# Cross-attention in a decoder: scores contracted over 64 rows on each half of the array, keys spread by ScalarE in place of GpSimd

## The reference

```python
x = x + attn_stack(layernorm(x))
# cross-attention: q from layernorm(x), k and v from ctx (16, 128, 128)
qh = (q @ Wq + bq)   # (16, heads 16, 128, 16)
kh = (k @ Wk + bk)
vh = (v @ Wv + bv)
scores = einsum('bhqd,bhkd->bhqk', qh, kh) * 16 ** -0.5
x = x + (softmax(scores) @ vh, heads joined) @ Wo + bo
x = x + experts(layernorm(x))
```

## Time and profile before

| | us |
|---|---|
| median of 3 runs | 3431.5 (3430.92 to 3431.95) |
| span of the profiled execution, first to last instruction | 3428.6 |
| cross-attention in it, from the first load to the last update | 2851.2 to 3101.5 |

### The profile page before, as it was taken

How to read it: one execution, slowest core, us unless ns; L and a number is a source line. 1 busy time by engine, 2 the same in 40 slices (tenths; PEclk the granted TensorE clock), 3 DMA queues, 4 the chain that set the end, 5 groups by cost and what they waited for, 6 DMA issues and landing times. The chain is left out here.

```text
span 3428.6 us, 44182 instructions
## 1 busy us (share of the span) xinstructions
PE 3029.2 (88%) x11560; PEld 2029.0 (59%) x11561; DVE 2711.6 (79%) x8902; ACT 1927.6 (56%) x2995; POOL 1323.7 (39%) x1039
## 2 busy tenths in 40 slices
PE   5698989898989898999899989998999976998995
PEld 4465656565656565666566655665566644776553
DVE  8879888988898889888988898889888834763111
ACT  4566666666666666666666666666666622442221
POOL 5325343534353435343534353435443323333002
PEclk9899999999999999999999999999999987997998
DMA  4001100100011001000100010001000001003312
GB/s 102 17 1 24 25 16 18 24 25 16 18 24 25 16 18 24 25 16 18 24 25 16 18 24 25 16 18 24 18 24 4 1 0 49 0 0 131 100 40 74
DMA packets 212286, 93.22 MB, mean 27 GB/s; under 512 B 146792, under 2 KB 207984, under 8 KB 212048
## 3 DMA queue, kind: packets, MB, share of 16 engines
q1 hardware_dynamic: 209408, 83.30, 9.6%
q0 software_dynamic: 2640, 7.21, 0.6%
HBM read 80.24 MB, written 10.22 MB: 26 GB/s over the span
## 5 line engine op out<-in xcount | busy, mean ns | idle before, releaser
L350 PE MATMUL PS<-XTHI,WHI 128*128 128x512 f32 x1536 | 672.6, 438 | 38.1 <-DVE EK L654 27.9
L285 POOL TENSOR_TENSOR INV<-INV,CE 128x512 f32<-128x512 f32 x256 | 305.9, 1195 | 984.1 <-DVE INV L697 984.1
L646 DVE SCALAR_TENSOR_TENSOR RK<-RK,EK 128x128 f32<-128x128 f32 x1024 | 599.6, 638 | 28.7 <-ACT RK L515 0.5
L351 PE MATMUL PS<-XTLO,WHI 128*128 128x512 f32 x1536 | 610.7, 398 | 0.0
L352 PE MATMUL PS<-XTHI,WLO 128*128 128x512 f32 x1536 | 609.9, 397 | 0.0
L398 PE MATMUL Y<-ATT,WO 128*128 128x512 f32 x1024 | 468.5, 612 | 59.8 <-POOL ATT L289 59.4
L398 PE MATMUL Y<-H,W2S 128*128 128x512 f32 x1024 | 465.9, 609 | 51.9 <-DVE R L708 50.4
L289 POOL TENSOR_TENSOR ATT<-INV,CC 128x512 f32<-128x512 f32 x256 | 316.7, 1237 | 195.5 <-PE Y L398 177.9
L398 PEld LDWEIGHTS Y<-ATT,WO 128*128 128x128 f32 x1024 | 197.7, 196 | 301.0 <-issue 298.2
L350 PEld LDWEIGHTS PS<-XTHI,WHI 128*128 128x128 f32 x1536 | 291.4, 190 | 133.2 <-issue 42.3
L398 PEld LDWEIGHTS Y<-H,W2S 128*128 128x128 f32 x1024 | 197.0, 195 | 290.4 <-issue 227.2
(11 more groups left out here) (195 smaller groups left out, 5440.7 us busy)
## 6 DMA issues: line engine op xcount, KB each, us to landing
STAGE<-L_attn_Wk SPq DMA_DIRECT2D x128, 64.0 KB, 2.1
STAGE<-L_attn_Wv SPq DMA_DIRECT2D x128, 64.0 KB, 2.1
STAGE<-L_attn_Wq SPq DMA_DIRECT2D x128, 64.0 KB, 2.1
WO<-L_attn_Wo SPq DMA_DIRECT2D x8, 1024.0 KB, 5.5
W2S<-L_attn_W SPq DMA_DIRECT2D x8, 1024.0 KB, 6.1
STAGE<-L_attn_W SPq DMA_DIRECT2D x64, 128.0 KB, 3.7
RAW<-L_ffn_r_gate SPq DMA_DIRECT2D x8, 512.0 KB, 3.5
RAW<-L_ffn_r_up SPq DMA_DIRECT2D x8, 512.0 KB, 3.6
```

The source lines that it names most:

```text
L285: nc.gpsimd.tensor_tensor(r3, r3, spread(CE[:, e, :], SEQ), ALU.mult).then_inc(att_s, 1)
L350: nc.tensor.matmul(out, whi[:, kc, :], xhi[:, kc, :], start=(kc == 0), stop=False)
L351: nc.tensor.matmul(out, whi[:, kc, :], xlo[:, kc, :], start=False, stop=False)
L646: ins = nc.vector.scalar_tensor_tensor(RK[:, p, seq(b)], RK[:, p, seq(b)], 0.0, EK[:, p, seq(b)], ALU.add, ALU.add, accum_out=SUMK[:, p, b ...
```

## The change

The scores now contract 64 rows, the four heads of one half: rows 0 to 63 with the first half of KX, rows 64 to 127 with the second, as two matmuls on two halves of the array's rows. KX so needs four copies of the keys instead of eight, and each row keeps its own head's copy among its four. ScalarE writes these copies straight from PSUM, as scale x keys + scale x bias, where the scale is a column of ones and zeros (PAIR, one column for each of four heads) and the bias a masked one (BKP). GpSimd's products, KT and the large mask are gone; VectorE makes PAIR from a small mask of GpSimd's, and BKP once the biases have landed. The scores now wait for ScalarE's keys and queries themselves.

```diff
+GROUPS = 2
+GH = CH // GROUPS
+GROUP = P // GROUPS
...
-        KT = sb("XKT", [P, 2, KD, P])
-        KX = sb("XKX", [P, 2, CH, SEQ])
+        KX = sb("XKX", [P, 2, KD, GH, SEQ])
...
-        S = ctx.enter_context(nc.psum_tensor("XS", [P, 2, CH * SEQ], F32))
+        S = ctx.enter_context(nc.psum_tensor("XS", [P, KD, GROUPS, GH * SEQ], F32))
...
-            def apart(i, j, c):
-                u = (2 * i + j) * KD + c
-                pool.wait_ge(kt, 2 * i + (j + 1))
-                if not (type(i) is int and u < 2):
-                    pool.wait_ge(s_mm, u - 1)
-                nc.gpsimd.tensor_tensor(KX[:, c, :, :], bcast(KT[:, j, c, :], CH), MASK[:, :, :], ALU.mult).then_inc(kx, 1)
...
             def scores(b, j, c):
                 u = b * KD + c
-                pe.wait_ge(kx, u + 1)
+                pe.wait_ge(kt, b + 1)
+                pe.wait_ge(qt, b + 1)
                 if not (type(b) is int and u < 2):
                     pe.wait_ge(sh, u - 1)
-                for hf in range(2):
-                    ins = nc.tensor.matmul(S[:, c, hf * 512:(hf + 1) * 512], QT[:, j, c, :],
-                                           KX[:, c, hf * 4:(hf + 1) * 4, :].rearrange("p h s -> p (h s)"),
-                                           start=True, stop=True)
+                for i in range(GROUPS):
+                    rows = slice(i * GROUP, (i + 1) * GROUP)
+                    ins = nc.tensor.matmul(S[:, c, i, :], QT[rows, j, c, :],
+                                           KX[rows, j, c, :, :].rearrange("p h s -> p (h s)"), start=True, stop=True)
                 ins.then_inc(s_mm, 1)
...
             def qk(b, j):
                 act.wait_ge(qk_mm, b + 1)
                 for c in range(KD):
-                    ins = nc.scalar.activation(KT[:, j, c, :], A[:, (2 + c) * P:(3 + c) * P], ACT.Identity,
-                                               bias=BK[:, c:c + 1])
+                    for h in range(GH):
+                        ins = nc.scalar.activation(KX[:, j, c, h, :], A[:, (2 + c) * P:(3 + c) * P], ACT.Identity,
+                                                   scale=PAIR[:, h:h + 1], bias=BKP[:, c, h:h + 1])
                 ins.then_inc(kt, 1)
...
+            dve.wait_ge(own_set, 2)
+            nc.vector.tensor_reduce(PAIR[:, :], OWN[:, :].rearrange("p (i h) -> p h i", h=GH), AX.X,
+                                    ALU.max).then_inc(pair_set, 1)
             prepare(0)
+            dve.wait_ge(pair_set, 1)
+            dve.wait_ge(bias_in, 64)
+            nc.vector.tensor_tensor(BKP[:, :, :], spread(BK[:, :], GH), bcast(PAIR[:, :], KD), ALU.mult).then_inc(bkp_set, 1)
             dve.wait_ge(r0, 1)
             dve.wait_ge(prep, 3)
             normed(0, 0)
             normed(1, 1)
             prepare(1)
-            dve.wait_ge(bias_in, 64)
             values(0, 0)
```

More of the change, by code:

```diff
@@ L872, in cross_attention @@
         BOX = sb("XBO", [P, D])
-        MASK = sb("XMASK", [P, CH, SEQ])
+        OWN = sb("XOWN", [P, CH])
+        PAIR = sb("XPAIR", [P, GH])
+        BKP = sb("XBKP", [P, KD, GH])
         HALF = sb("XHALF", [P, SEQS])
@@ L899, in cross_attention @@
         w_in, bias_in = (sem(n) for n in ("xw_in", "xbias_in"))
-        set0, ones_set, v0, r0, mask_set, kx = (sem(n) for n in ("xset0", "xones_set", "xv0", "xr0", "xmask_set", "xkx"))
+        set0, ones_set, v0, r0, own_set, pair_set, bkp_set = (
+            sem(n) for n in ("xset0", "xones_set", "xv0", "xr0", "xown_set", "xpair_set", "xbkp_set"))
         prep, z, mx, sh, rd, o, v1, ob, upd = (
@@ L928, in _ @@
             nc.gpsimd.memset(HALF[:, :], -0.5).then_inc(set0, 1)
-            nc.gpsimd.memset(MASK[:, :, :], 1.0).then_inc(set0, 1)
+            nc.gpsimd.memset(OWN[:, :], 1.0).then_inc(set0, 1)
             nc.gpsimd.memset(V1[:, :, :, XK:XK + 1], 1.0).then_inc(ones_set, 1)
             pool.wait_ge(set0, 2)
[L933 to L937, removed]
+            nc.gpsimd.affine_select(out=OWN[:, :], in_=OWN[:, :], compare_op=ALU.is_ge, fill=0.0, base=0,
+                                    pattern=[[-XK, CH]], channel_multiplier=1).then_inc(own_set, 1)
+            pool.wait_ge(own_set, 1)
+            nc.gpsimd.affine_select(out=OWN[:, :], in_=OWN[:, :], compare_op=ALU.is_ge, fill=0.0, base=XK - 1,
+                                    pattern=[[XK, CH]], channel_multiplier=-1).then_inc(own_set, 1)
             def rstd(k):
@@ L947, in _ @@
             rstd(0)
-            pool.wait_ge(mask_set, 2)
-            def apart(i, j, c):
-                u = (2 * i + j) * KD + c
-                pool.wait_ge(kt, 2 * i + (j + 1))
-                if not (type(i) is int and u < 2):
-                    pool.wait_ge(s_mm, u - 1)
-                nc.gpsimd.tensor_tensor(KX[:, c, :, :], bcast(KT[:, j, c, :], CH), MASK[:, :, :], ALU.mult).then_inc(kx, 1)
-            apart(0, 0, 0)
-            apart(0, 0, 1)
-            rstd(1)
[L960 to L965, removed]
+            rstd(1)
         def step(i, j):
@@ L1135, in _ @@
             inputs(0, 0)
+            act.wait_ge(bkp_set, 1)
             qk(0, 0)
@@ L1160, in shifted @@
                 dve.wait_ge(s_mm, u + 1)
-                scores = S[:, c, :].rearrange("p (h s) -> p h s", h=CH)
+                scores = S[:, c, :, :].rearrange("p i (h s) -> p (i h) s", h=GH)
                 nc.vector.tensor_reduce(MX[:, c, :], scores, AX.X, ALU.max).then_inc(mx, 1)
```

## The result

The change makes the kernel slower: 3483.4 us median (3479.0 to 3488.4) beside 3431.2 us for the kernel before on the same chip, a ratio of 1.016 with a 95% interval of 1.014 to 1.018.

A forecast was written before the change was run, and what follows sets the result against it. It took a loop closing through TensorE, ScalarE and VectorE, 12.80 us a sequence, as the bound. Terms 34.5 - 6 + 1.5 - 0.4 + 7 = +36.6 us gave 3468; range 3442 to 3502, with 0.19 outside.

The forecast's parts named there:

- ScalarE's evictions, +34.5: Key evictions in the cross-attention loop, eight in place of two, lengthen the path by 2.3 us in each of 15 sequences.
- The choice of a second operand that costs as much as the first: Each key eviction's scale column adds 95 ns, as the bias does, so the eight stand 0.35 us apart.
- The scores, -6: Score matmuls on 64 rows free 0.43 us ahead of the projection, 14 times; the other chunk frees nothing.
- The choice of three pass times: A chunk's four score passes take 1.29 us, only the middle two overlapping; bounds 0.86 and 1.72.
- the slack at the projection: 0.54 us between the turned output's copy and the projection, while TensorE streams scores; the most the scores could free.
- The rival of a faster kernel: TensorE is the true bound and both score chunks run in 0.86 us: -27.5 us, 3404; chance 0.08.
- Ahead of the loop, +1.5: The masked bias on VectorE waits for the bias vectors, so the values come later: 1.5 us, bounds 0 and 2.5.
- GpSimd and VectorE, 0: Dropping GpSimd's products speeds VectorE's normalisation, but VectorE then waits for the projection: no time gained.
- The clock, +7: TensorE's new wait after narrow matmuls brings clock falls in three sequences of four, not two: +7 us, bounds -14 and +14.
- Rival 2: The clock falls for most of the loop, two falls a sequence: +71 us, 3502; stretch 3485 to 3520, chance 0.19.
- the forecast's own stretch: The main forecast's interval for the changed kernel's time, 3458 to 3485 us, chance 0.50.
- the signs that were to show the forecast wrong: Transposes still some 4.6 us after the first, pace set outside this loop, or granted clock in the loop below 0.8.

The follow-up runs named there:

- kernel 2: The kernel before plus six ScalarE activations with scale and bias columns into an unread tile, 128-row scores and GpSimd's products kept; 3470.6 us, ratio 1.010 to 1.016.
- kernel 9: 64-row scores alone (GpSimd still writing the keys) plus one idle 128x256 matmul ahead of the first transposes, against the kernel before; 3421.9 us, ratio 0.997 to 0.999.
- kernel 3: The changed kernel plus two idle 128x512 matmuls in TensorE's wait ahead of the values; 3458.2 us, ratio to the kernel before 1.006 to 1.013.
- Kernel 1: The kernel before with only the 64-row scores; GpSimd still writes the keys, four copies, and ScalarE keeps two key evictions; 3427.9 us, ratio 0.998 to 1.002.
- kernel 12: The changed kernel plus two idle 128x512 matmuls ahead of the values and one idle 128x256 ahead of the first transposes; 3456.8 us, ratio 1.007 to 1.011.
- kernel 10: The kernel before, 128-row scores, plus one idle 128x512 matmul ahead of the first transposes; 3435.1 us, ratio 1.002 to 1.004.

## Why the prediction was right, and where it was off

The direction and the main mechanism held: ScalarE's evictions are on the path, and most of the loss is theirs (kernel 2). The sum of 36.6 us came out as 52.2, by its own terms so:

- **ScalarE's evictions, +34.5.** Measured 3.25 - 1.02 = 2.23 us a sequence, 33.5 in all. The choice of a second operand that costs as much as the first held: the eight start (2.90 - 0.47) / 7 = 0.35 us apart by their rows (mean duration 0.47), and without the column (2.17 - 0.38) / 7 = 0.26. The Trainium skill (ScalarE: Activation LUTs, "What ACT_TABLE_LOAD costs") gives about 93 ns to such an operand; the two spacings differ by 0.09 us, which agrees.
- **The scores, -6.** The size held, by luck. The choice of three pass times was wrong: the four passes take two, 1.13 us at full clock beside 1.97. Still the loop gained only 14.55 - 12.73 - 2.23 = -0.41 us a sequence at full clock, -6 in all: the slack at the projection was 0.54 at most, and 0.05 is left of it (kernel 9: copy's end 2949.41, projection 2949.46), while the projection itself now takes 1.13 us in place of 1.03. The rival of a faster kernel had the matmul nearly right (0.84 saved in each chunk beside its 0.86) and its effect wrong. The Trainium skill (TensorEngine Tiling (Array Packing), "Theoretical Speedup") promises up to two times; the rows show half the pass times and 1.97 / 1.13 = 1.7 times for a chunk. The Trainium skill (TensorEngine Tiling (Array Packing), "Key Properties") says that a change of mode drains the array; the rows leave room for a small cost of it. The scores start 0.31 us behind the turned output in kernel 9 (2947.92 to 2948.23), 0.22 before (2969.06 to 2969.28), and the next matmul 1.06 - 2 x 0.43 = 0.20 beyond two pass times (2952.99 to 2954.05), where 0.08 lay beyond four (2961.77 to 2963.57). That is some 0.2 us a chunk; whether a drain is its cause, no run shows.
- **Ahead of the loop, +1.5.** From the first load's issue to the first transposes 32.6 us (2848.41 to 2880.99), before 31.8 (2851.24 to 2883.02): +0.8, inside its bounds.
- **GpSimd and VectorE, 0.** The normalisation takes 0.41 us, as foreseen, and VectorE then waits 4.40 us for the projection: nothing gained.
- **The clock, +7.** This step failed. I expected one fall in three sequences of four and bounded it by one in each; there are two in each, which cost 2.52 us a sequence in place of 0.85 (kernel 3): 1.67 x 15 = +25, beyond the term's upper bound of 14. Rival 2 named the two falls and over-priced them: they cost 2.52 / 2 = 1.3 us each, not 1.83. (That 1.83 compares a shorter sequence with a longer neighbour: 14.49 - 12.80 = 1.69.)

33.5 - 6 + 0.8 + 25 = 53.3, beside 53.7 measured in the stage and 52.2 between the medians. The three large terms are parts of the same difference of paces, so that they add up to it is no test of each. The term of the clock is mis-sized because I counted the falls that a wait adds at one place. The changed kernel has two: the new wait, and the narrow products followed by scores that now pass in half the time. Kernel 1 shows the second without the first, kernel 3 takes the first away. Why the second comes in every sequence of one kernel and in few of another is open.

That the median lies in the forecast's own stretch, 3458 to 3485, is in part luck: it does so by 1.6 us, two of the four executions lie beyond it (3486.9 and 3488.4), and what pushed it there were the two falls a sequence of rival 2. Of the signs that were to show the forecast wrong, the granted clock came to its bound, 0.80 in nearly every sequence. The chance outside the range was also set a little low: 3502 to 3520 is half of rival 2's stretch, not a third.

## What to carry to other kernels

Before moving work onto an engine with idle time, find what stands behind it in that engine's order: ScalarE was busy for 43% of the loop, and its extra 2.2 us still lengthened each sequence in full. A shorter matmul on TensorE pays only as long as what it leaves doesn't let the clock fall; look at the granted clock just behind the place that got faster. Where TensorE waits anyway, idle work that just fits the wait can hold the clock (kernels 3 and 9), though it need not (kernel 12); where it doesn't wait, it buys nothing (kernel 10).

## What the runs showed of the hardware that was not expected

Passes of the two row halves overlap fully although they are issued half by half: their weight loads come in pairs, 0.85 us apart at the lower clock, as these rows ahead of the loop of the changed kernel show.

```profile
2876.25 0.34 PEld L1005 LDWEIGHTS XS<-XKX,XQT 64*128 64x128 f32 x2 [0.51 <-issue]
2877.10 0.34 PEld L1005 LDWEIGHTS XS<-XKX,XQT 64*128 64x128 f32 x2 [0.51 <-issue]
```

And the clock answers to small things: 0.43 us of idle matmul in each sequence (two passes, half as wide as the scores') took most falls out of kernel 1, and 0.73 us less of ScalarE's work in each sequence saved 41 us where its duration accounts for 11.
